# Seven inverse square roots in a two-block decoder: from ScalarE's Ln and Exp to a power on GpSimd

## The reference

```python
x = x + linear_attention(layernorm(x))
x = x + cross_attention(layernorm(x), ctx)
x = x + experts(layernorm(x))
x = x + state_space_scan(layernorm(x))
x = x + cross_attention_with_bias(layernorm(x), ctx)
x = x + quantised_feed_forward(layernorm(x))
```

## Time and profile before

| | |
|---|---|
| median of 3 runs | 706.07 us (704.36, 706.07, 727.68) |
| the profiled execution | 706.75 us, its span 705.0 us |
| PE | 562.9 us busy, 80% of the span |
| DVE | 480.3 us, 68% |
| ACT | 269.0 us, 38% |
| POOL | 118.7 us, 17%, 79 instructions |
| chain that ended last | PE 64%, DVE 23%, issue 5%, ACT 5%, DMA 1%, POOL 1% |
| Ln of the norms, L222 | 13, 191 to 210 ns |
| Exp of the norms, L223 | 13, 205 to 209 ns |
| table loads on ACT | 20, 1283 ns each: 8 at L978, 6 at L217, 3 at L965, 1 each at L222, L223 and L1507 |

### The profile page before, as it was taken

How to read it: one execution, slowest core, us unless ns; L and a number is a source line. 1 busy time by engine, 2 the same in 40 slices (tenths; PEclk the granted TensorE clock), 3 DMA queues, 4 the chain that set the end, 5 groups by cost and what they waited for, 6 DMA issues and landing times.

```text
span 705.0 us, 8929 instructions
## 1 busy us (share of the span) xinstructions
PE 562.9 (80%) x3166; PEld 323.3 (46%) x3170; DVE 480.3 (68%) x1181; ACT 269.0 (38%) x453; POOL 118.7 (17%) x79
## 2 busy tenths in 40 slices
PE   4795679999799999999995446665659999999334
PEld 2242356666356666666664102222246555555203
DVE  5489837675457366666555699999756666665686
ACT  2522034555443233243242465455113333334174
POOL 6345100000000000300000067777600000000000
PEclk9888679999979999999998657878859999999655
DMA  4000060000100000000000000000010000000001
GB/s 114 0 4 1 0 209 1 1 2 2 39 0 1 0 1 1 1 4 1 1 0 1 0 0 0 0 1 1 0 37 1 1 1 1 1 1 2 0 0 31
DMA packets 10095, 8.20 MB, mean 12 GB/s; under 512 B 1634, under 2 KB 9124, under 8 KB 10052
## 3 DMA queue, kind: packets, MB, share of 16 engines
q1 hardware_dynamic: 10052, 7.64, 3.8%
HBM read 6.98 MB, written 0.52 MB: 11 GB/s over the span
## 4 chain that ended last, share of the span: by engine, by line
PE 64%; DVE 23%; issue 5%; ACT 5%; DMA 1%; POOL 1%; POOLq 0%; another core or an unknown queue 0%; SPq 0%; DVEq 0%; ACTq 0%
PE PS L920 16%; PE PS L603 10%; PE PS L931 8%; PE PS L640 7%; PE PS L653 5%; DVE VA L1370 4%; PE PS L636 3%; PE PS L588 3%; DVE PS L1351 3%; DVE PS L1363 2%; DVE sums L487 2%; PE PS L620 2%; PE PS L282 2%; PE PS L663 1%; DVE E L483 1%
## 5 line engine op out<-in xcount | busy, mean ns | idle before, releaser
L920 PE MATMUL PS<-XNT,KSA 128*128 128x512 f32 x256 | 121.0, 610 | 1.2 <-ACT XNT L960 0.8
L755 ACT ACTIVATE E<-PS 128x512 f32<-128x512 f32 x128 | 73.1, 597 | 108.1 <-PE PS L640 80.3
L603 PE MATMUL PS<-KP,QP 32*128 32x256 f32 x512 | 109.2, 398 | 0.0
L1125 DVE TENSOR_TENSOR E<-E,PS 128x512 f32<-128x512 f32 x64 | 43.8, 686 | 57.8 <-ACT E L978 57.5
L640 PE MATMUL PS<-QM,KP 32*128 32x256 f32 x512 | 81.3, 399 | 0.0
L792 DVE CUSTOM_DVE_ANT_0 SCR<-PS,KSA 128x256 f32<-128x256 f32 x128 | 48.7, 421 | 44.3 <-PE PS L603 44.3
L978 ACT ACTIVATE E<-PS 128x512 f32<-128x512 f32 x64 | 38.2, 597 | 106.3 <-PE PS L920 104.5
L603 PEld LDWEIGHTS PS<-KP,QP 32*128 32x128 f32 x512 | 69.7, 184 | 13.1 <-issue 9.0
L931 PEld LDWEIGHTS PS<-KSA,E 128*128 128x128 f32 x512 | 62.1, 192 | 16.3 <-issue 15.1
L920 PEld LDWEIGHTS PS<-XNT,KSA 128*128 128x128 f32 x256 | 46.6, 195 | 45.3 <-issue 42.6
L931 PE MATMUL PS<-KSA,E 128*128 128x128 f32 x512 | 62.4, 275 | 1.3 <-DVE XN L1116 1.3
(11 more groups left out here) (249 smaller groups left out, 839.2 us busy)
## 6 DMA issues: line engine op xcount, KB each, us to landing
KSA<-in_w SPq DMA_DIRECT2D x2, 1024.0 KB, 6.8
X<-in_x SPq DMA_DIRECT2D x1, 512.0 KB, 3.8
SCR<-in_ctxT SPq DMA_DIRECT2D x1, 512.0 KB, 7.0
SCR<-in_fside SPq DMA_DIRECT2D x1, 512.0 KB, 4.7
out_x<-X SPq DMA_DIRECT2D x8, 64.0 KB, 1.5
wx<-in_w_x SPq DMA_DIRECT2D x1, 384.0 KB, 8.0
wself<-in_w_self SPq DMA_DIRECT2D x1, 256.0 KB, 8.4
KSA<-in_w1T SPq DMA_DIRECT2D x1, 256.0 KB, 10.2
```

The costliest lines, as they stand in the source:

```text
L603: ins = pe.matmul(score_bank(n, i)[:, q * S:(q + 1) * S], QP[rows(i), g, t:t + P], KP[rows(i), g, b * S:(b + 1) * S], start=True, stop=Tru ...
L755: act.activation(slot(m, j), weight_bank(m, j), ACT.Exp).then_inc(sig("exps"), 1)
L920: ins = pe.matmul(bank(2 * (g % 3) + o), w[:, e, c * P:(c + 1) * P], XNT[:, tokens_of(p)], start=True, stop=True)
L1125: dve.tensor_tensor(E6[:, g % 4, :], E6[:, 4 + g % 2, :], bank(2 * (g % 3) + 1), ALU.mult)\
```

## The change

The roots of norms 2 to 8 are taken out of ScalarE's queue, together with the four table loads `exp_and_ln` that stood ahead of norms 4 to 7 inside the experts. Each becomes one GpSimd instruction, `rs = ve ** exponent`, where `exponent` is a new tile of 128x8 numbers filled once with -0.5. The signals are the same: the instruction waits for `ve` and signals `root`. VectorE's and TensorE's queues are not edited. Norms 0, 1 and 9 to 12 stay on ScalarE, and so does the `exp_and_ln` after the last Silu.

In GpSimd's queue the fill and the powers of norms 2, 3, 4 and 5 stand behind `tri` and ahead of the bias conversion; the wait for `x_res` (the residual of the first block's cross attention) that stood there is gone, and the wait for `ve` of norm 2 takes its place. The powers of norms 6, 7 and 8 stand between `NEGT` and the scan.

```diff
+        exponent = sb("exponent", [P, NT])
...
+        def norm_power(pool, k, s=slice(0, NT)):
+
+            pool.wait_ge(sig("ve"), k + 1)
+            pool.tensor_tensor(rs[:, s], ve[:, s], exponent[:, s], ALU.pow).then_inc(sig("root"), 1)
...
         def experts_scalar(act, ch):
             act.wait_ge(sig("router_in"), 32)
-            norm_root(act, ch, 3, tiles_of(0))
             keys_take(act, 1, 3, 5)
...
-                if p + 1 < PASSES and n == 3:
-                    exp_and_ln(act)
-                    norm_root(act, ch, 3 + p + 1, tiles_of(p + 1))
...
-                if p == 3 and n == 6:
-                    exp_and_ln(act)
-                    norm_root(act, ch, 7, tiles_of(0))
...
         # block gpsimd
-            x_ready(pool, 2)
+            ch.link(pool.memset(exponent[:, :], -0.5))
+            norm_power(pool, 2)
+            norm_power(pool, 3, tiles_of(0))
+            norm_power(pool, 4, tiles_of(1))
+            norm_power(pool, 5, tiles_of(2))
             pool.wait_ge(sig("fside_in"), 16)
             pool.wait_ge(sig("w_quantised"), 2)
...
             pool.tensor_scalar(NEGT, PAD, -NEG_X1, None, ALU.mult).then_inc(sig("neg"), 1)
+            norm_power(pool, 6, tiles_of(3))
+            norm_power(pool, 7, tiles_of(0))
+            norm_power(pool, 8, tiles_of(1))
             scan_pool(pool)
...
         # block scalar
             keys_take(act, 1, 1, 5)
-            norm_root(act, ch, 2)
             keys_take(act, 1, 2, 3)
             experts_scalar(act, ch)
-            norm_root(act, ch, 8, tiles_of(1))
             half_take(act, 1, 5)
```

## The result

The changed kernel took 708.08 us in the median of five runs (707.99 to 709.37), beside 706.07 us for the kernel before; the ratio is 1.005, with a 95% interval of 1.0029 to 1.0071. A second series gave 1.0039 (1.002 to 1.0059). The changed kernel is slower by 2 to 5 us, which is less than 1% and more than the 0.4 us of the forecast. The time lies inside the predicted range, just above the forecast's own range of 705.5 to 708. The profiled execution took 707.99 us, its span is 706.3 us.

A forecast was written before the change was run, and what follows sets the result against it. The prediction took TensorE alone to bound the expert stage. Its five parts summed as 0 + 0.4 + 0 + 0 + 0 = +0.4 us on the 706.07 us median, giving 706.5 us, range 702.8 to 712.

The forecast's parts named there:

- Part 1: Covered roots of norms 4 to 7 inside the passes: ScalarE gives back 12.2 us, gain and cost priced 0.
- Part 2: Exposed roots of norms 2, 3 and 8: ScalarE's 1.67 us go, three hand-overs plus powers come, +0.4 us.
- P: Length of one power on GpSimd, not in the trace; taken as 0.5 us, between 0.2 and 1.0 us.
- formula of the prediction: Cost at norms 2, 3 and 8: 3 x (power length + 0.18 us hand-over) - 1.67 us.
- rival (a): Slow power on GpSimd, 1 to 5 us, computed in software per column; 713.3 us at 2.78 us; chance 0.17.
- stretch at 0.50: TensorE at its 1.2 GHz level behind the 3.14 us idle ahead of 192.47 us; changed length would mean prediction wrong.
- Parts 3 and 5: GpSimd's queue order delays nothing, and sharing SBUF access with VectorE costs nothing: 0 each.
- part 4: ScalarE's queue: key copies end some tenths sooner, but the transpose at 192.47 us waits for VectorE: 0.
- Rival (b): Powers above 5.1 us make exposed norms cost over 14.1 us; about 721.5 us at 5.5 us; chance 0.05.
- Rival (c): One-off stall at the first power, at norm 2: 707.8 us, or 712.5 by the skill's figure; chance 0.08.
- Rival (e): ScalarE was on the path after all, and 12.2 us come back: 694 us; chance 0.02.
- Rival (d): TensorE's clock moves around its idle time ahead of the experts: 702.5 us or 708.5 us; chance 0.11.

The follow-up runs named there:

- inner powers alone: Against the kernel before, only norms 4 to 7 became powers on GpSimd; norms 2, 3 and 8 stayed on ScalarE: ratio 0.9963.
- doubled powers: Changed kernel with every power computed twice in a row, the first result unused: ratio 1.0174 to the kernel before.
- filled version with norm 12: Kernel before with GpSimd powers for norms 4 to 7 and 12, plus three unused products in TensorE's pause ahead of the experts: ratio 0.9947.
- filled pair: Unused products in TensorE's pause ahead of the experts: five in the changed kernel, ratio 0.9998; three in the kernel before, ratio 0.9958.
- version with norm 12: Kernel before with GpSimd powers for norms 4 to 7 and 12, norms 2, 3 and 8 staying on ScalarE: ratio 0.992 without filler, 0.9947 with.

## Why the prediction was right or wrong

**Part 1** was right: a power inside a pass costs nothing, rounds stay at 5.22 us, and the 12 us that ScalarE gives back buy nothing. The inner powers alone show both.

**Part 2** is the term that was mis-sized. I took P = 0.5 us, because the smallest conversion takes 0.20. It was 1.67 us for 8 columns and 1.01 for 4. With these the formula of the prediction gives 1.67 + 1.01 + 1.01 + 3 x 0.18 - 1.67 = +2.6 us; the traces show +2.5, and the doubled powers another 3.6 where the same sizes give 3.7. The place and the mechanism were right; the case that happened is the low end of rival (a). That the time grows with the columns, as (a) has it, fits the slope of 0.165 us; that GpSimd computes in software is shown by no run. The hand-over, taken as 0.18 us, was 0.19, 0.12 and 0.17 us. Two signs that the prediction had named for being wrong came true: the power took over 1 us, and the stretch at 0.50 changed its length.

**Parts 3 and 5** held, and no wait in the traces speaks against part 4. The power of norm 6 began 1.86 us after NEGT; `mix` beside a power took 1.12 us as without one.

**Rival (b)** did not happen; P would have had to be three times as long. **Rival (c)** is excluded by the doubled powers, 1.67 us for the first and 1.64 for the second. The Trainium skill (GPSIMD Engine Reference, Instruction dispatch) gives about 6 us for the first call of freshly loaded code. No such cost is in this trace; whether a power is code of that kind, no run shows. **Rival (e)** is excluded by the inner powers alone: with the work off ScalarE, the way from norm 2's variance to the scan took 216.80 us instead of 216.77.

**Rival (d)** did happen, and I had under-rated it. I had expected one low stretch to move by a few tenths of a pause; three more appeared, worth 5.1 us in the profiled execution, while elsewhere 5.6 us were won (the first and last stretch of the table). The first stretch of the table ends before any power. The two low stretches at 231 and 241 need neither kind of power by itself: they stand in a trace without exposed powers and in one without inner powers. The two traces without any power on GpSimd don't have them, so that powers play no part at all is not shown. What brings them is open. Of the nine traces used here that have the narrow groups, five have a low stretch behind both groups and four behind neither; the three traces with the one-row products left out or made wide have none. The place is certain. That the one-row products are the cause is likely and not shown: where four of nine lack the stretches anyway, three traces without them could be chance.

That the total came so near is in part luck. The first comparison's 1.005 is 3.5 us, the second's 2.8; both intervals contain the 2.5 us of waits. But in the profiled execution the clock cost 5.1 us in one part and gave 5.6 us in others, and elsewhere such shifts did not cancel: the twelve executions of the filled version with norm 12 took 700.07 to 709.64 us. So the 2.5 us are shown by the waits and by the doubled powers at their own place, not by the totals.

What stays open: why of two executions with the same instructions on TensorE one loses the clock behind the thin groups and the other doesn't. The position in time doesn't order them simply: the first group began at 224.91, 225.56, 228.24, 228.50 and 233.55 us in the five traces with low stretches, and at 227.62, 227.95, 229.26 and 229.61 in the four without. It also stays open what share of the totals' scatter this is.

## What to carry to other kernels

A tiny operation on GpSimd is not small because its tile is: find out its price before it goes on a chain. Moving one that already has cover costs nothing, and by itself it also buys nothing. What a table load costs on an idle ScalarE is nothing; look for the one where the next engine really waits (here norm 12, between Gelu and the end). A total that agrees with the expectation is no proof either: the filled pair agreed to 0.3 us, while its traces had no such difference in the expert stage. When a difference is below 1%, compare stretches between the same events in both traces, and look at the granted clock of each, before you ascribe it to the edit.

## What the runs showed of the hardware that was not expected

- A power of two SBUF tiles on GpSimd: 1.01 us for 128x4 and 1.67 us for 128x8, 0.165 us per column between the two, while a product of 512 columns took 1.16 us there, 0.0023 us per column. So a column of a power costs some 70 times a column of a product.
- TensorE's clock fell to its 1.2 GHz level for about 3.4 us (granted 0.57 and 0.58 over 4 us) with TensorE busy all the time, behind groups of 3.1 us that alternate 128-row and one-row contractions. This happened in five of nine traces with eight narrow one-row products, and in none of the three with two wide ones or without any.
- With unused products in TensorE's pause of 3 to 5 us the first unit behind it took 1.98 us instead of 3.64 to 3.78. In the changed kernel and in the version with norm 12 the granted clock stayed at 1.00 from 186 to 200 us; in the kernel before, where the filler came behind 2.00 us without work, it fell to 0.66 from 191 to 196 us and was back at 1.00 for the first unit.
- Up to norm 2's variance TensorE, VectorE and ScalarE have the same work in all versions, and yet it was ready anywhere from 184.8 to 188.2 us in the traces.
